# Last expert layer of an eight-block network: the shared expert's up products with the weights stationary over 512 tokens, in high and low parts, and the routing ranks ahead of them

## The chip, the cores and the metric

One core of one Trainium2 chip runs the whole program as a single launch. The metric is device time in microseconds, the median of a few executions; less is better. The engines that matter here are TensorE (PE, with its weight loads shown apart as PEld), VectorE (DVE), ScalarE (ACT), GpSimd (POOL) and SyncE (SP, which only issues DMAs). They run side by side and wait for one another through semaphores.

## The reference, cut to what matters

Four times an attention block and a feed-forward block are added to x, each behind a layer norm and a gate. The change touches the last feed-forward block (B S = 1024 tokens of D = 256 features; E = 8 experts, two per token, hidden width 512, and one shared expert that every token passes), and the third and last attention block only in so far as it prefetches.

```python
x = hidden_states.reshape(-1, 256)                     # 1024 tokens, after the layer norm
shared_out = silu_and_mul(x @ shared_gate_up) @ shared_down      # (256 -> 2*512), (512 -> 256)
probs = softmax(x @ gate_w)                            # 8 experts
topk_w, topk_i = top_k(probs, 2);  topk_w = topk_w / sum(topk_w)
combine = sum(one_hot(topk_i, 8) * topk_w[..., None], axis=1)
for wg, wd, cw in experts:                             # 8 of them
    moe_out += cw[:, None] * (silu_and_mul(x @ wg) @ wd)
return moe_out + shared_out
```

`silu_and_mul` splits its input into a gate and an up half of 512 and gives silu(gate) * up.

## The kernel before, in words

`routed` (from L1742) is the last block. Its order is written out by hand: one program for each engine, and semaphores between them. Tokens come in T = 8 tiles of 128. The work on PE is a list of 31 items: n = 0 to 7 are the 8 token tiles through the shared expert, n = 8 to 30 are NT = 23 tiles of 128 rows, each of one routed expert, gathered by expert.

First DVE writes the normalised tokens XE, PE turns them (L1995) into four PSUM banks, ACT and DVE copy these to XTF (features on partitions; it lives in the tensor XN), and PE computes the router's logits LG (L2003). DVE then runs the routing in small steps: softmax, comparisons of all pairs of experts, and then four functions that are threaded between the shared items by the table `BETWEEN`: `rank` (which experts are chosen), `weigh` (their weights), `place` (the row of a table in DRAM, rows3, for each token and choice), `owners` (which expert owns each of the 23 tiles). `rank` feeds a small count on PE (`count`, L2014 and L2016), which `place` needs. When `place` is done, POOL scatters XE to rows3 with 16 indirect DMAs (L1841), and when all have landed SP loads the first six tiles XB from rows3 (L1821). An expert tile can't start before its rows are back.

One item on PE is: `up` (L2027: 4 products, a 128x128 block of tokens as the stationary side and 512 columns of weights moving, plain fp32, into the two PSUM banks GU), `turn_x` of the next tile where that is a routed one (L2036), `down` of the item before (L2054: 4 products with 256 moving columns into DN), and `turn_h` (L2044: 4 transposes of the hidden tile into HP). ACT makes silu of the gate bank (HG, L1865) and DVE multiplies it by the up bank (HF, L1959). `turn_h` is needed since HF has tokens on partitions and `down` wants the hidden features there; ACT copies its result to HT (L1871). `down` of a shared item is added to X (`finish`, L1971); `down` of a routed item is scaled to YB (L1976), and POOL adds it to the output in DRAM by an indirect DMA (L1848), after X itself has been stored (L1824).

In the trace every plain fp32 product stands as two records with a weight load each. So `x8` at L2027 is one item's four products.

All nine weight blocks (the shared one, index E, first; 1.5 MB each) are loaded by SP at the start of the block (L1814, L1816); PE waits for the eighth expert's before the first routed item.

`mm3` (L95 to L97) is used elsewhere in the program: it makes a product from parts, a high part (the value rounded to fp32r, a reduced fp32 format of the matmul) and a low part (what is left of it), by three fp32r matmuls, high x high, high x low, low x high. Each of these is one record.

`plain_attend` (L1135) is attention 2 and 3; on POOL it spreads keys (L1331, L1332), and after that POOL is idle in attention 3.

## Time and profile before

| what | value |
|---|---|
| median of 3 runs | 1010.23 us (1009.95 to 1011.49) |
| the profiled execution's own time | 1009.22 us |
| its span | 1007.4 us |
| PE busy over the span | 933.2 us, 93% |
| the last block (`routed`) | from 796.7 us to the end |
| its shared items on PE (L2027 from XN, first start) | from 805.3 us |
| its first routed item on PE | at 859.4 us |

The span is what the trace covers; 1.8 us lie around it. A time in a view counts from the start of the span. A view of the chain of waits shows the work that ended last, followed back from the end; a timeline shows single instructions of an engine; a view by windows sums busy time and gives the granted clock of TensorE in each stretch (1.00 is full speed). "issue" and "remote" as a releaser mean that the profile has no event of another engine for the end of that wait.

### The profile page before, as it was taken

What the parts mean: (1) busy time and instruction counts of PE and PEld (TensorE: products, weight loads), DVE (VectorE), ACT (ScalarE), POOL (GpSimd) and SP (SyncE); (2) the same over time, 40 slices, a digit from 0 to 9 for tenths busy, and PEclk for the clock granted to TensorE, in tenths of its full rate; (3) what the DMA queues carried; (4) which work ended last, traced back from release to release, by engine and by line L of the source; (5) the groups of instructions that cost most, each with busy time, mean ns of one, the idle gap of its engine ahead of it and who ended that gap; (6) DMA issues with size and microseconds to landing.
All of it is one profiled execution on the core that took longest, in us unless ns stands there. A gap on an engine that the chain in (4) does not pass through costs nothing. (4 is left out here: it accounts for less than half of the span.)

```text
span 1007.4 us, 15178 instructions
## 1 busy us (share of the span) xinstructions
PE 933.2 (93%) x5006; PEld 696.5 (69%) x5022; DVE 571.2 (57%) x1069; ACT 345.4 (34%) x612; POOL 424.3 (42%) x341
## 2 busy tenths in 40 slices
PE   7999998988899999999979988898799898999996
PEld 4899996966566666667758966786378654666554
DVE  6788886668343443443579887677777451222221
ACT  3454543410033333343424435344154231212111
POOL 5787883030378888674402230530350014122222
PEclk9999999987899999999989999999999899999999
DMA  8321110049345445656520010100000294222210
GB/s 306 129 83 52 44 44 1 2 162 409 96 78 86 77 74 84 148 76 169 170 84 1 2 37 0 38 1 1 11 1 1 95 428 162 57 43 43 36 30 10
DMA packets 38595, 84.84 MB, mean 84 GB/s; under 512 B 9741, under 2 KB 27533, under 8 KB 36014
## 3 DMA queue, kind: packets, MB, share of 16 engines
q1 hardware_dynamic: 22062, 64.56, 18.3%
q0 software_dynamic: 16176, 19.31, 11.6%
q8 instruction: 41, 0.67, 0.3%
q14 instruction: 28, 0.23, 0.1%
q10 hardware_dynamic: 288, 0.07, 0.0%
HBM read 71.23 MB, written 20.68 MB: 91 GB/s over the span
## 5 line engine op out<-in xcount | busy, mean ns | idle before, releaser
L2546 PE MATMUL ffn_GU<-ffn_W,ffn_XTB 128*128 x252 | 90.0, 479 | 3.0 <-DVE ffn_XTB L2451 1.9
L1848 POOL DMA_INDIRECT out_x<-ffn_YB,ffn_XB x23 | 35.8, 1557 | 119.2 <-DVE ffn_YB L1976 117.2
L2027 PE MATMUL ffn_GU<-ffn_W,ffn_XTB 128*128 x184 | 85.0, 605 | 0.0
L2253 POOL DMA_INDIRECT kept_MARKED<-scratch_rows,kept_IDX x63 | 62.4, 991 | 52.3 <-DMA scratch_rows<-ffn_WEIGHT 33.4
L2435 DVE TENSOR_TENSOR ffn_GB<-ffn_GU,ffn_BIAS 128x352 f32<-128x352 f32 x63 | 33.1, 525 | 86.6 <-PE ffn_GU L2546 72.5
L2546 PEld LDWEIGHTS ffn_GU<-ffn_W,ffn_XTB 128*128 128x128 f32 x252 | 43.2, 189 | 35.5 <-issue 21.2
L2054 PE MATMUL ffn_DN<-ffn_W,ffn_HT 128*128 (+1 forms) x248 | 60.3, 387 | 5.6 <-issue 4.9
L2577 PE MATMUL ffn_DN<-ffn_W,ffn_HT 96*128 x252 | 64.8, 379 | 0.0
L2291 ACT ACTIVATE ffn_HG<-ffn_GB 128x176 f32<-128x176 f32 x63 | 22.0, 350 | 115.9 <-DVE ffn_GB L2435 70.0
L1965 DVE COPY ffn_XTB<-ffn_XP 128x256 f32<-128x256 f32 x23 | 9.8, 425 | 86.6 <-PE ffn_XP L2036 86.6
L2027 PEld LDWEIGHTS ffn_GU<-ffn_W,ffn_XTB 128*128 128x128 f32 x184 | 33.1, 189 | 36.0 <-issue 33.6
L2054 PEld LDWEIGHTS ffn_DN<-ffn_W,ffn_HT 128*128 128x128 f32 x248 | 46.0, 193 | 14.7 <-issue 9.6
L356 POOL TENSOR_TENSOR attn_RP<-attn_RP,attn_RS 128x512 f32<-128x512 f32 x32 | 40.6, 1290 | 33.8 <-DVE attn_RS L523 33.8
L1865 ACT ACTIVATE ffn_HG<-ffn_GU 128x512 f32<-128x512 f32 x31 | 18.5, 597 | 88.2 <-PE ffn_GU L2027 84.5
L2577 PEld LDWEIGHTS ffn_DN<-ffn_W,ffn_HT 96*128 96x128 f32 x252 | 43.0, 190 | 3.5
L351 POOL TENSOR_TENSOR attn_WS_lo<-attn_W,attn_WS_hi 128x896 fp32r<-128x896 f32 (+2 forms) x24 | 41.6, 1746 | 5.2 <-ACT attn_WS_hi L427 5.2
L1084 POOL TENSOR_TENSOR attn_PROB<-XN,attn_SM 128x1024 f32<-128x1024 f32 x8 | 15.2, 1904 | 61.3 <-DVE attn_SM L1107 61.3
L95 PE MATMUL attn_QB<-attn_XT_hi,attn_C_hi 128*128 128x512 f32 x96 | 38.5, 401 | 2.3 <-DVE attn_XT_lo L565 2.3
L1871 ACT ACTIVATE ffn_HT<-ffn_HP 128x512 f32<-128x512 f32 x31 | 18.5, 597 | 62.7 <-PE ffn_HP L2044 51.9
L97 PE MATMUL attn_QB<-attn_XT_hi,attn_C_lo 128*128 128x512 f32 x96 | 37.5, 391 | 0.0
L96 PE MATMUL attn_QB<-attn_XT_lo,attn_C_hi 128*128 128x512 f32 x96 | 37.5, 391 | 0.0
L1959 DVE TENSOR_TENSOR ffn_HF<-ffn_GU,ffn_HG 128x512 f32<-128x512 f32 x31 | 21.4, 692 | 26.2 <-ACT ffn_HG L1865 23.2
(529 smaller groups left out, 2520.1 us busy)
## 6 DMA issues: line engine op xcount, KB each, us to landing
ffn_W<-in_f_w SPq DMA_DIRECT2D x9, 1536.0 KB, 6.2
ffn_W<-in_f_w SPq DMA_DIRECT2D x16, 608.0 KB, 18.3
attn_W<-in_L_pairs SPq DMA_DIRECT2D x7, 1088.0 KB, 4.9
scratch_rows<-in_rows_empty SPq DMA_DIRECT2D x1, 2967.0 KB, 13.2
ffn_XB<-scratch_rows SPq DMA_DIRECT2D x23, 129.0 KB, 2.1
ffn_BIAS<-in_f_bias SPq DMA_DIRECT2D x1, 2816.0 KB, 15.3
kept_STAGE<-in_f_w SPq DMA_DIRECT2D x1, 2048.0 KB, 9.6
kept_STAGE<-in_L_pairs SPq DMA_DIRECT2D x2, 768.0 KB, 9.5
```

The source lines that it names most:

```text
L95: pe.matmul(out, a[0], b[0], start=first, stop=False)
L96: pe.matmul(out, a[0], b[1], start=False, stop=False)
L97: return pe.matmul(out, a[1], b[0], start=False, stop=last)
L351: pool.tensor_tensor(WS[1][:, SECTIONS[c]], W[:, SECTIONS[c]], WS[0][:, SECTIONS[c]].bitcast(F32), ALU.subtract).then_inc(w_lo[c], 1)
L356: pool.tensor_tensor(RP[:, q, g, :], RP[:, q, g, :], RS[:, g, 1 - q, :], ALU.add).then_inc(rope_add, 1)
L1848: pool.indirect_dma_start(out[:, :], bass.IndirectOffsetOnAxis(ap=XB[:, i % NB, D:D + 1].bitcast(I32), axis=0), YB[:, i % 3, :], None, bou ...
L2027: last = pe.matmul(GU[:, m, :], x, weights(e, k * 2 * HID3 + m * HID3, HID3), start=k == 0, stop=k == KD - 1)
L2054: last = pe.matmul(DN[:, n % 2, 0:D], HT[:, n % 2, c * P:(c + 1) * P], weights(e, UPW + c * D, D), start=c == 0, stop=c == HID3 // P - 1)
L2253: pool.indirect_dma_start(XB[:, i % NB, :], None, DR["rows0"][:, :], bass.IndirectOffsetOnAxis(ap=IDX[:, i:i + 1], axis=0)).then_inc(rows_ ...
L2435: dve.tensor_tensor(GB[:, n % 2, :], GU[:, n % 2, 0:2 * HID], BIAS[:, bass.ds(e * (2 * HID), 2 * HID)], ALU.add).then_inc(biased, 1)
L2546: last = pe.matmul(GU[:, n % 2, 0:2 * HID], XTB[:, i % 2, k * P:(k + 1) * P], flat[:, bass.ds(e * WIDTH0 + k * 2 * HID, 2 * HID)], start=k ...
L2577: last = pe.matmul(DN[:, n % 2, 0:D], HT[0:rows, n % 2, j * P:(j + 1) * P], w, start=j == 0, stop=j == len(parts) - 1)
```

## The change

1. The shared expert's up weights (128x2048 fp32) are no longer part of W. They are loaded (RAW) at the start of attention 3's block by SP, and split into a high and a low part by two POOL instructions after POOL's last key work there. The parts lie in the space of a tensor, STAGE, that is free by then. W keeps the 8 experts; the shared down weights (128x1024) are a tile of their own, WD.
2. XT, high and low parts of the turned tokens: ACT writes four high parts from the PSUM banks (128x512 each), POOL the four low parts.
3. A shared step is no longer a token tile. There are 8 steps s = 4 h + c: half h of the tokens (512) and chunk c (128) of the hidden features. The weights' 128x128 blocks are stationary, 512 tokens move, in `mm3` form: 2 banks x 2 feature chunks x 3 = 12 matmuls. The result has hidden features on partitions, so `turn_h` and the copy to HT go for the shared part. Two pairs of banks alternate, GU and HP with XP. The hidden tiles are kept in eight places that are free at that time (XB, HF, CMP, HT).
4. `shared_down(t)` is as `down` was: 4 fp32 products with 256 columns per token tile.
5. Order on PE: steps 0, 1, the count, steps 2, 3; then four times a step and one `shared_down`; then four `shared_down`; then `turn_x(8)` and the routed items. On DVE `rank` comes ahead of the first product with silu, and `place` ahead of the third. SP loads XB only after four `shared_down` too.
6. The first routed item has no `down` of an item before it, and `turn_x(8)` has no `up` beside it.

The diff, without the parts that only rename or redirect (waits counted from T, sizes of tiles):

```diff
-        def plain_attend(... normalised=0):
+        def plain_attend(... normalised=0, next_shared=None):
...
+                    else:
+                        @block.sync
+                        def _(sp):
+                            next_shared["load"](sp)
...
+                        if next_shared:
+                            next_shared["halve"](pool)
...
+        def shared_weights(ctx, PARTS):
+            RAW = sbuf(ctx, "RAW", [P, KD * 2 * HID3])
+            loaded, halves = sem(ctx, "shared_loaded"), sem(ctx, "shared_halves")
+            def load(sp):
+                sp.dma_start(RAW[:, :], A["f3_w"][E3][:, 0:KD * 2 * HID3]).then_inc(loaded, 16)
+                sp.wait_ge(loaded, 16)
+            def halve(pool):
+                pool.wait_ge(loaded, 16)
+                pool.tensor_copy(PARTS[0], RAW[:, :]).then_inc(halves, 1)
+                pool.wait_ge(halves, 1)
+                pool.tensor_tensor(PARTS[1], RAW[:, :], PARTS[0].bitcast(F32), ALU.subtract).then_inc(halves, 1)
...
+                HIDDEN = [LATER[:, c * HALF:(c + 1) * HALF] for c in range(3)] + [HF[:, :], CMP[:, 0, :], CMP[:, 1, :], HT[:, 0, :], HT[:, 1, :]]
+                PAIRS = ((GU[:, 0, :], GU[:, 1, :]), (HP[:, :], XP[:, :]))
...
-                        sp.dma_start(W[:, E, :], A["f3_w"][E]).then_inc(shared_in, 16)
+                        sp.dma_start(WD[:, :], A["f3_w"][E][:, UPW:WIDTH]).then_inc(shared_in, 16)
...
                         sp.wait_ge(scattered, 16 * 2 * T)
+                        sp.wait_ge(down_done, T // 2)
...
+                        for j in range(4):
+                            pool.wait_ge(xt_b if j % 2 else xt_a, j // 2 + 1)
+                            pool.wait_ge(xt_hi, j + 1)
+                            pool.tensor_tensor(XT[1][:, j % 2, half(j)], XTF[:, j % 2, half(j)], XT[0][:, j % 2, half(j)].bitcast(F32), ALU.subtract).then_inc(xt_lo, 1)
...
-                        for j in (0, 2):
+                        for j in range(4):
                             act.wait_ge(xt_turned, j + 1)
-                            act.activation(XTF[:, 0, half(j)], NBANK[j], ACT.Copy).then_inc(xt_a, 1)
+                            if j % 2 == 0:
+                                act.activation(XTF[:, 0, half(j)], NBANK[j], ACT.Copy).then_inc(xt_a, 1)
+                            else:
+                                act.wait_ge(xt_b, j // 2 + 1)
+                            act.activation(XT[0][:, j % 2, half(j)], NBANK[j], ACT.Copy).then_inc(xt_hi, 1)
...
-                        BETWEEN = {0: rank, 1: weigh, 2: place, 3: owners}
+                        rank()
+                        shared_full(0)
+                        weigh()
+                        shared_full(1)
+                        place()
+                        shared_full(2)
+                        shared_full(3)
+                        owners()
...
+                        def shared_up(s):
+                            h, c = divmod(s, 4)
+                            pe.wait_ge(xt_hi, 2 * h + 2)
+                            pe.wait_ge(xt_lo, 2 * h + 2)
+                            if s >= 2:
+                                pe.wait_ge(h_full, s - 1)
                             for m in range(2):
                                 for k in range(KD):
+                                    at = slice(k * 2 * HID3 + m * HID3 + c * P, k * 2 * HID3 + m * HID3 + (c + 1) * P)
+                                    last = mm3(pe, PAIRS[s % 2][m], (WS[0][:, at], WS[1][:, at]),
+                                               [x[:, k, h * HALF:(h + 1) * HALF] for x in XT], first=k == 0, last=k == KD - 1)
+                            last.then_inc(up_done, 1)
+                        def shared_down(t):
+                            h, q = divmod(t, T // 2)
+                            pe.wait_ge(h_full, 4 * h + 4)
+                            if t >= 2:
+                                pe.wait_ge(shared_added, t - 1)
+                            for c in range(HID3 // P):
+                                last = pe.matmul(DN[:, t % 2, 0:D], HIDDEN[4 * h + c][:, q * P:(q + 1) * P], WD[:, c * D:(c + 1) * D], start=c == 0, stop=c == HID3 // P - 1)
+                            last.then_inc(down_done, 1)
...
+                        shared_up(0)
+                        shared_up(1)
+                        count()
+                        shared_up(2)
+                        shared_up(3)
                         pe.wait_ge(shared_in, 16)
+                        for s in range(4, T):
+                            shared_up(s)
+                            shared_down(s - 4)
+                        for t in range(4, T):
+                            shared_down(t)
+                        pe.wait_ge(experts_ready, 1)
+                        turn_x(T)
+                        pe.wait_ge(w_in, 16 * E)
```

How instructions stand on PE at the start of the shared part, before the change (LG are the logits, GU the bank pair of `up`, HP the turned hidden tile, PF the count):

```order
L2003 MATMUL ffn_LG<-ffn_RW,XN 128x8 x16
L2027 MATMUL ffn_GU<-ffn_W,XN 128x512 x4
L2044 MATMUL ffn_HP<-IDENT,ffn_HF 128x128 x4
L2027 MATMUL ffn_GU<-ffn_W,XN 128x512 x4
L2054 MATMUL ffn_DN<-ffn_W,ffn_HT 128x256 x4
L2014 MATMUL ffn_PF<-ffn_CHOSEN,ffn_TRI 128x72
```

And there after the change (shared_up_11063 and shared_up_11064 are the high and the low part of the weights; the three rows L95 to L97 stand four times for one step, twice on each bank of its pair):

```order
L2060 MATMUL ffn_LG<-ffn_RW,XN 128x8 x16
L95 MATMUL ffn_GU<-ffn_XT_hi,shared_up_11063 128x512
L96 MATMUL ffn_GU<-ffn_XT_lo,shared_up_11063 128x512
L97 MATMUL ffn_GU<-ffn_XT_hi,shared_up_11064 128x512
...
L95 MATMUL ffn_HP<-ffn_XT_hi,shared_up_11063 128x512
...
L97 MATMUL ffn_XP<-ffn_XT_hi,shared_up_11064 128x512
L2069 MATMUL ffn_PF<-ffn_CHOSEN,ffn_TRI 128x72
```

The transposes HP and the `down` between the first two items are gone, and the second step, on HP and XP, stands right behind the first one.

On DVE, from the last comparison (CMP) to the slots, before the change (HF is the product with silu, PR and XE the ranks and weights, TE and SLOT the placing):

```order
L1914 TENSOR_TENSOR ffn_CMP<-ffn_PR 128x512
L1959 TENSOR_TENSOR ffn_HF<-ffn_GU,ffn_HG 128x512
L1918 TENSOR_TENSOR ffn_CMP<-ffn_CMP,ffn_BEFORE 128x512
L1919 TENSOR_TENSOR ffn_CMP<-ffn_CMP 128x512
L1920 TENSOR_REDUCE ffn_PR<-ffn_CMP 128x64
L1922 TENSOR_SCALAR ffn_CHOSEN<-ffn_PR 128x64
L1959 TENSOR_TENSOR ffn_HF<-ffn_GU,ffn_HG 128x512
L1971 SCALAR_TENSOR_TENSOR X<-ffn_DN,GATE,X 128x256
L1925 SCALAR_TENSOR_TENSOR ffn_PR<-ffn_PR 128x64
```

And after the change (the first product with silu now goes to space of XB):

```order
L1956 TENSOR_TENSOR ffn_CMP<-ffn_PR 128x512
L1960 TENSOR_TENSOR ffn_CMP<-ffn_CMP,ffn_BEFORE 128x512
L1961 TENSOR_TENSOR ffn_CMP<-ffn_CMP 128x512
L1962 TENSOR_REDUCE ffn_PR<-ffn_CMP 128x64
L1964 TENSOR_SCALAR ffn_CHOSEN<-ffn_PR 128x64
L1999 TENSOR_TENSOR ffn_XB<-ffn_GU,ffn_HG 128x512
L1967 SCALAR_TENSOR_TENSOR ffn_PR<-ffn_PR 128x64
```

`rank` has moved ahead of the first product, and between `rank` and `weigh` one product stands where there were a product and a sum into X.

On PE where the routed items begin, before the change:

```order
L2027 MATMUL ffn_GU<-ffn_W,XN 128x512 x4
L2036 MATMUL ffn_XP<-IDENT,ffn_XB 128x128 x2
L2054 MATMUL ffn_DN<-ffn_W,ffn_HT 128x256 x4
L2044 MATMUL ffn_HP<-IDENT,ffn_HF 128x128 x4
L2063 TENSOR_LOAD ffn_EI
L2063 ISA x2
L2027 ISA
L2027 MATMUL ffn_GU<-ffn_W,ffn_XTB 128x512
```

And after it:

```order
L97 MATMUL ffn_XP<-ffn_XT_hi,shared_up_11064 128x512
L2093 MATMUL ffn_DN<-ffn_WD,ffn_XB 128x256 x3
L2093 MATMUL ffn_DN<-ffn_WD,ffn_HF 128x256
L2093 MATMUL ffn_DN<-ffn_WD,ffn_CMP 128x256 x2
L2093 MATMUL ffn_DN<-ffn_WD,ffn_HT 128x256 x2
...
L2112 MATMUL ffn_XP<-IDENT,ffn_XB 128x128 x2
L2149 TENSOR_LOAD ffn_EI
L2149 ISA x2
L2101 ISA
L2101 MATMUL ffn_GU<-ffn_W,ffn_XTB 128x512
```

The transposes XP of the first routed tile now stand behind all shared work, right before the product that needs them; before, they stood ahead of a `down` and a `turn_h`.

## Rows read from the trace of the kernel before

**Rows 1.** Chain that ended last, last block: start us, us, what.

```profile
805.48 5.25 PE ffn_GU L2027 x8
...
812.86 3.44 PE ffn_GU L2027 x8
816.29 1.73 PE ffn_DN L2054 x8
...
844.56 4.87 issue
849.44 3.48 PE ffn_DN L2054 x8
...
859.38 3.70 PE ffn_GU L2027 x8
863.08 0.22 PE ffn_XP L2036 x2
...
865.02 0.44 PE ffn_HP L2044 x4
865.46 3.58 PE ffn_GU L2027 x8
```

**Rows 2.** Timeline of ACT and DVE: start us, us, instruction [idle before <-releaser].

```profile
811.45 0.69 DVE L1959 TENSOR_TENSOR ffn_HF<-ffn_GU,ffn_HG 128x512 f32<-128x512 f32 x1 [3.08 <-ACT ffn_HG L1865]
...
845.24 0.48 DVE L1971 SCALAR_TENSOR_TENSOR X<-ffn_DN,GATE,X 128x256 f32<-128x256 f32 x1 [4.92 <-issue]
848.79 0.60 ACT L1871 ACTIVATE ffn_HT<-ffn_HP 128x512 f32<-128x512 f32 x1 [9.19 <-remote]
```

**Rows 3.** Windows: us, busy us (instructions) PE, PEld, DVE, ACT, POOL, PEclk, DMA, GB/s.

```profile
805.30:810.70 5.40, 5.40 (x10) 2.05 (x9) 2.52 (x8) 1.54 (x2) 0.00 (x0) 0.68 1.00 422
812.80:844.60 31.80, 31.76 (x118) 18.60 (x116) 11.48 (x34) 7.77 (x11) 13.20 (x14) 1.00 0.82 336
849.40:853.60 4.20, 4.16 (x13) 3.36 (x14) 1.18 (x2) 0.61 (x2) 0.00 (x0) 0.59 0.57 150
```

**Rows 4.** Timeline of PE in attention 3, second and last of 24 fp32r products.

```profile
735.43 0.40 PE L96 MATMUL attn_TR<-layer_XT_lo,kept_WQ_hi 128*128 128x512 f32 x1
...
740.57 0.40 PE L97 MATMUL attn_OP<-layer_XT_hi,kept_WQ_lo 128*128 128x512 f32 x1
```

**Rows 5.** Timeline of DVE: first and last instruction of rank, weigh and place.

```profile
812.06 0.68 DVE L1918 TENSOR_TENSOR ffn_CMP<-ffn_CMP,ffn_BEFORE 128x512 f32<-128x512 f32 x1
814.22 0.20 DVE L1922 TENSOR_SCALAR ffn_CHOSEN<-ffn_PR 128x64 bf16<-128x64 f32 x1
818.46 0.22 DVE L1925 SCALAR_TENSOR_TENSOR ffn_PR<-ffn_PR 128x64 f32<-128x64 f32 x1
820.15 0.29 DVE L1933 TENSOR_REDUCE ffn_XE<-ffn_WEIGHTS 128x16 f32<-128x128 f32 x1
824.33 0.16 DVE L1937 TENSOR_SCALAR ffn_TE<-ffn_PF 128x8 f32<-128x8 f32 x1
826.42 0.17 DVE L1947 CAST ffn_SLOT<-ffn_SLOTF 128x16 int32<-128x16 f32 x1
```

**Rows 6.** Timeline of POOL and SP: first and last of 16 scatters, loads of XB.

```profile
827.44 1.03 POOL L1841 DMA_INDIRECT scratch_rows<-ffn_XE,ffn_SLOT  x1 [26.97 <-DVE ffn_SLOT L1947]
...
846.62 0.97 POOL L1841 DMA_INDIRECT scratch_rows<-ffn_XE,ffn_SLOT  x1 [0.30 <-issue]
849.09 3.89 SPq L1821 DMA_DIRECT2D ffn_XB<-scratch_rows  x6
```

**Rows 7.** The tile XB, the load that was issued at 849.09 us.

```profile
DMA to landing us min/median/max: 2.2/2.2/2.2
```

**Rows 8.** POOL's own DMA queue, 831 to 832 us: packets, MB, share.

```profile
q0 software_dynamic: 11, 0.05, 11.3%
```

**Rows 9.** Waits of POOL: instruction <- what it waited for: us, times, longest.

```profile
POOL ffn_ONEB L1829 <- POOLq L1184: 47.9, 1, 47.9
```

**Rows 10.** The page, costliest groups: xcount | busy us, mean ns | idle before.

```profile
L356 POOL TENSOR_TENSOR attn_RP<-attn_RP,attn_RS 128x512 f32<-128x512 f32 x32 | 40.6, 1290 | 33.8 <-DVE attn_RS L523 33.8
```

More of the change, by code:

```diff
@@ L1132, in _, with plain_attend @@
                         add(T - 1)
-        def plain_attend(tag, gate, CW, QO, MASKH, CWS, WQ, VB, following=None, next_weights=None, normalised=0):
+        def plain_attend(tag, gate, CW, QO, MASKH, CWS, WQ, VB, following=None, next_weights=None, normalised=0, next_shared=None):
             with ExitStack() as ctx:
@@ L1739, in _, with routed @@
                         keep_busy(pe, SP[:, :], 20)
-        def routed(gate):
+        def routed(gate, WS):
             E, NT, NB, ROW = E3, TILES3, 6, ROW3
@@ L1746, in routed @@
             with ExitStack() as ctx:
-                W = sbuf(ctx, "W", [P, E + 1, WIDTH])
+                W = sbuf(ctx, "W", [P, E, WIDTH])
+                WD = sbuf(ctx, "WD", [P, WIDTH - UPW])
+                XT = split(ctx, "XT", [P, KD, B * S])
                 XE = sbuf(ctx, "XE", [P, 2, T, ROW])
@@ L2017, in count, with up @@
                             last.then_inc(counted, 1)
-                        def up(n, e):
-                            if n > 0:
-                                pe.wait_ge(h_full, n)
-                            if n >= T:
-                                pe.wait_ge(x_out, n - T + 1)
+                        def shared_up(s):
[4 more added lines that the diff above has]
+                                pe.wait_ge(h_full, s - 1)
                             for m in range(2):
                                 for k in range(KD):
-                                    x = XTF[:, k, n * P:(n + 1) * P] if n < T else XTB[:, n % 2, k * P:(k + 1) * P]
-                                    last = pe.matmul(GU[:, m, :], x, weights(e, k * 2 * HID3 + m * HID3, HID3), start=k == 0, stop=k == KD - 1)
+                                    at = slice(k * 2 * HID3 + m * HID3 + c * P, k * 2 * HID3 + m * HID3 + (c + 1) * P)
[10 more added lines that the diff above has]
+                            last.then_inc(down_done, 1)
+                        def up(n, e):
+                            pe.wait_ge(h_full, n)
+                            pe.wait_ge(x_out, n - T + 1)
+                            for m in range(2):
+                                for k in range(KD):
+                                    last = pe.matmul(GU[:, m, :], XTB[:, n % 2, k * P:(k + 1) * P], weights(e, k * 2 * HID3 + m * HID3, HID3), start=k == 0, stop=k == KD - 1)
                             last.then_inc(up_done, 1)
@@ L2683, in program @@
         phase[0] = "ffn3_"
-        routed(7)
+        routed(7, SHARED)
 def rope_table(length, dim):
```

72 lines of the change are left out of this document (42 added, 30 removed).

## The prediction

> **What bounds the kernel now.** I read the chain of waits first. In the last block it is PE nearly all the way: an item's `up` takes 3.44 us, its `down` 1.73, its transposes 0.44 [rows 1], and PE was busy 31.76 of 31.80 us from 812.80 to 844.60 at full clock [rows 3]. So every matmul that goes from the shared part shortens the path. Two pieces of the chain are not of that kind. The first item took 5.25 us, at a mean granted clock of 0.68 [rows 1, 3]: part of it ran at 1.2 GHz. And at 844.56 PE stood still for 4.87 us, with "issue" as the reason, after which one `down` took 3.48 instead of 1.73 us, at a mean clock of 0.59 [rows 1, 3].
>
> Then I read the timeline of ACT and DVE beside that gap. The waiting `down` needed HT, which ACT wrote at 848.79 after an idle time of 9.19 us put down to "remote"; DVE's sum into X came at 845.24 after 4.92 us, put down to "issue" [rows 2]. PE's matmuls that both wait for stood in the chain ahead of 844.56 [rows 1]. So two engines got on late by several microseconds for a reason that the trace doesn't name. It falls into the time of the scatters, 827.44 to 847.59 [rows 6]. I call it the hiccup; with its slow clock it costs 4.87 + (3.48 - 1.73) + about 0.2 for the transposes behind it = 6.8 us.
>
> Last, the routing, which isn't on the path but must be ready for the first routed item: the slots were ready at 826.59 [rows 5], the scatters ran from 827.44, SP issued the XB loads at 849.09 [rows 6], and the first landed 2.2 us later [rows 7], at 851.3. PE came to that item at 859.38 [rows 1]: 8 us of slack.
>
> **The change part by part.** I compare the stretch of PE from 805.48 to 865.46, the start of the second routed `up` [rows 1]: 59.98 us. Behind it nothing is changed.
>
> Before, in that stretch: `up` 5.25 + 7 x 3.44 = 29.33; `up` of the first routed item 3.70; `down` 8 x 1.73 = 13.84; transposes of hidden tiles 9 times, 8 x 0.44 and 0.9 more for the slower ones, 4.4; `turn_x` 2 x 0.22; count 0.2; the wait of the first item for silu and product, 810.73 to 812.20, 1.4; the hiccup's 4.87 + 1.75. Sum 59.9.
>
> Step (a), the products. An fp32r product of 128x512 starts every (740.57 - 735.43) / 22 = 0.234 us [rows 4]. A step has 12, so 2.80 us; eight would take 22.4. A token tile's `up` had 8 records of 0.43. That is three passes in place of four, less the pitch's 0.02 each. The first step begins slow, as the first item did: that was 5.25 - 3.44 = 1.81 us late, so some 3.6 us ran at the lower level. In 3.6 us go 8 products of 0.43 (half rate), then 4 of 0.234: 4.5 us. All: 4.5 + 7 x 2.80 = 24.1, against 29.3. Gain 5.2.
>
> Step (b), what goes with the turned layout: eight groups of transposes (3.8 us) and the wait of 1.4 us, which the second pair of banks fills with step 1. Gain 5.3.
>
> Step (c), the downs: 8 x 1.73, the stationary side and the 256 columns are as before. `shared_down(3)` (1.73 us) covers silu (0.60) and product (0.69) of the last step [rows 2], which `shared_down(4)` needs: with two hand-overs of 0.06 that is 1.4 us, so nothing waits. Each `shared_down` waits for the sum into X two before it, 0.48 us of DVE [rows 2] in 1.73. Nought.
>
> Step (d), what is added at the border. `turn_x(8)` has no `up` beside it: the transposes (0.22 [rows 1]), the copy XTB (as long as DVE's other 128x256 pass, 0.48 [rows 2]) and two or three hand-overs of 0.06 make 0.85 us, 0.65 more than 0.22. The first routed item has no `down` behind it to cover silu and product: 1.4 us. Its `up` is 3.65, 0.05 less than before. Loss 2.0.
>
> Step (e), the hiccup. If it is gone, 6.8 us more.
>
> New stretch: 24.1 + 13.84 + 0.2 + 0.85 + 3.65 + 0.22 + 1.4 + 0.44 = 44.7. The gain is 59.98 - 44.7 = 15.3 us, of which 8.5 are work and bubbles and 6.8 the hiccup.
>
> Step (f), are the rows back? DVE is idle for 3.08 us before 811.45 [rows 2], so `rank` can start at 808.4. It takes 2.36 us (812.06 to 814.42), `weigh` 1.98 (818.46 to 820.44), `place` 2.26 (824.33 to 826.59) [rows 5]. PE ends step 0 at about 810.0, step 1 at 812.8, the count at 813.0. DVE: `rank` to 810.8, product to 811.5, `weigh` to 813.5, product 1 to 814.2, `place` to 816.5. That is 10 us earlier than 826.59. The scatters keep POOL 20.15 us plus 0.85 before, as in rows 6: last issue over at 837.5. SP issued the XB loads 1.5 us after that [rows 6], so 839.0, and the first lands at 841.2. PE is through its shared work at 805.48 + 24.1 + 0.2 + 13.84 = 843.6. So rows are there 2.4 us early: PE still sets the time, though the slack has shrunk from 8 us. SP's added wait, for four `shared_down`, is over at about 836.6, before the scatters are. What is queued behind it on SP are only the XB loads and the store of X.
>
> The scatters now fall into the load of the expert weights. There only 11 packets with 0.05 MB went through POOL's queue in one microsecond [rows 8], while a scatter is 0.13 MB and is issued every 1.28 us. From both sides: with no slowing the loads are issued at 839.0. If no scatter moves until the weights are in, 2.1 MB follow behind them. The weights are about 14 MB, 1 MB less than before, at 422 GB/s and a DMA share of 1.00 [rows 3], so in at about 831; the 2.1 MB take 5 us at that rate and 10 at half of it, and the loads are issued between 839 and 842.5. I take 839.0, since the issue by POOL, one in 1.28 us, was the slower part before. At the upper end the first tile lands at 844.7 and PE waits 1.1 us.
>
> The Trainium skill, DMA: Bandwidth & Descriptors, section Queues, rings and completion order, says that each DMA engine serves its queues in turn, packet by packet. By that rule the scatters are neither shut out nor ahead; the sum would stay at 839. The trace agrees as far as both queues moved packets in the same microsecond [rows 8].
>
> Step (g), edits at nothing. The load of RAW and POOL's two instructions of 128x2048 lie in attention 3, where POOL was idle for 47.9 us before this block [rows 9]; they need about 10 us of it, by elements from POOL's 128x512 pass of 1.29 us [rows 10]. If DVE were slowed by them, as two engines at the same memory can be, it could cost up to their own 10 us; DVE's softmax steps are on that block's path. I take 0. ACT's four and POOL's four new passes before the first step run beside the logits (801.9 to 805.5): ACT, at 0.60 a pass, is done at about 803.5, and the two low parts that step 0 needs, at 1.29 us each [rows 10] from about 801, at 803.6. I take 0; if that cover is gone, 1 us.
>
> **Forecast.** Span 1007.4 - 15.3 = 992.1; with the 1.8 us around it 993.9. The median of the runs shown, 1010.23, is 1.0 above the profiled execution; so 995.
>
> **The rivals.**
> A. The hiccup stays. It came while scatters were under way [rows 2, 6], and these are all still there. For it: two engines were late at once for no reason in the program, so the cause is outside the instructions that moved. Against: it came once in 16 scatters, and the change moves the scatters to a time in which PE does other things. In the new order most PE work of that time doesn't need ACT (four `shared_down` in a row), so it may also be partly hidden. Time: 995 + 6.8 = 1001.8 at most. Chance 0.33.
> B. The rows come late and PE waits at `turn_x(8)`: the scatters are stretched beyond the bound above, or POOL is held up by a full queue. For it: before, 6 scatters had been issued when the weights were in, now 11 or 12 will be. If POOL could issue only one in 2 us until 831, 9 would be left, over at 843, and the rows land at 846.7: 3 us of waiting, and a slow clock behind it as at 849.44 (another 1.9). Against: POOL's gap of 0.30 us stayed the same under the load [rows 6]. Time 995 + 5 = 1000. Chance 0.10.
> C. On the other side: PE's clock. If the new order leaves PE at the lower level, each product takes 0.43 us, 2.36 us more for a step, and each `shared_down` 3.48 instead of 1.73 [rows 1]. Over the whole shared part that is 7 x 2.36 + 8 x 1.75 = 30.5 us, and the time 1025. It decides from half of it on: over 15 us of loss, or some 31 us of the stretch at the lower level, is slower than before. Against: from 812.80 on the clock was 1.00 with PE as dense as it will be [rows 3]. For: the first item's 0.68 shows that the level is low on entry [rows 3]. Chance 0.04. The Trainium skill, TensorE: Matmul & The Clock Gate, section Part 1: The HAM clock gate, calls the throttled state the default that activity releases; by it the sum stays, since activity doesn't fall.
> D. The products don't run at the pitch of rows 4, or the split costs attention 3 up to its 10 us: 995 + 4 to 10, up to 1005. Chance 0.06.
> The forecast itself, hiccup gone or hidden: 0.47, with its own range 992.5 to 997.5.
>
> **How the numbers follow.** A, B and D lie between 999 and 1003, the forecast between 992.5 and 997.5. From 992 to 1002.5 I leave out C, the worst of D, and some below. Faster by over 0.2% (about 2 us, what can be told from no change here) is all but C and mishaps: 0.95; no change 0.01; slower 0.04.
>
> **What would show it.** In the changed profile: L95 to L97 on GU, HP and XP at a start-to-start of 0.23 us, 96 in all; the first scatter at 817 to 818 and the XB loads at 839; the first routed `up` at about 844.5 and the second near 850; the slots at about 816.5; clock 1.00 from 810 on; no idle PE over 1.5 us after that. Any gap of PE over 3 us with "issue" or "remote" on ACT or DVE is rival A; a wait of `turn_x(8)` for XB is B; L95 to L97 at 0.4 us beyond the first step is C; longer DVE steps in attention 3 are D. If the stretch to the second routed `up` is over 48 us without such a gap, my sum is wrong.

## The result, and the profile after

| what | value |
|---|---|
| median of 13 runs | 1002.68 us (1000.30 to 1008.75) |
| the kernel before, 13 runs | 1011.33 us (1008.94 to 1018.39) |
| ratio | 0.9922, 95% interval 0.9903 to 0.9941 |
| the profiled execution's own time, its span | 1000.98 us, 999.2 us |

Faster by 8.7 us, not by the 15.3 that were forecast; 1002.68 lies just above the range's end of 1002.5, and 0.9 above rival A's 1001.8. (The 13 runs of before have a median 1.1 us above that of the three runs that the forecast started from.) I call *the stretch* what the prediction compared: PE from the first shared product to the start of the second routed `up`. Before it took 59.98 us [rows 1]. After the change it is 55.3 us, where 44.7 were forecast.

The chain of waits of the changed kernel (start us, us, what) answers to rows 1:

```profile
802.14 0.63 PE ffn_GU L95
802.76 0.43 PE ffn_GU L96
...
807.03 0.43 PE ffn_GU L97
...
824.56 0.70 DVE ffn_CMP L1999
825.30 12.50 another core or an unknown queue
837.83 0.61 ACT ffn_HG L1903
...
839.87 0.70 DVE ffn_HT L1999
840.62 9.65 PE ffn_DN L2093 x32
...
851.35 3.69 PE ffn_GU L2101 x8
...
857.31 3.70 PE ffn_GU L2101 x8
```

Two things are to be seen. The first step's products start 0.43 us apart, where those of rows 4 are 0.234 us apart: half the rate. And the chain leaves PE for 12.5 us, for something that the profile has no name for. The timeline of PE, ACT and DVE of the same time shows what it was (start us, us, instruction [idle before <-releaser]):

```profile
828.26 1.46 PE L2093 MATMUL ffn_DN<-ffn_WD,ffn_XB 128*128 128x256 f32 x6
834.97 0.38 PE L2093 MATMUL ffn_DN<-ffn_WD,ffn_HF 128*128 128x256 f32 x1 [0.53 <-issue]
840.62 2.08 PE L2093 MATMUL ffn_DN<-ffn_WD,ffn_CMP 128*128 128x256 f32 x4 [5.27 <-DVE ffn_HT L1999]
842.48 1.91 PE L2093 MATMUL ffn_DN<-ffn_WD,ffn_HT 128*128 128x256 f32 x4
851.35 3.69 PE L2101 MATMUL ffn_GU<-ffn_W,ffn_XTB 128*128 x8 [0.88 <-DVE ffn_XTB L2011]
```

```profile
837.83 0.60 ACT L1903 ACTIVATE ffn_HG<-ffn_GU 128x512 f32<-128x512 f32 x1 [13.30 <-remote]
```

```profile
827.17 0.48 DVE L2017 SCALAR_TENSOR_TENSOR X<-ffn_DN,GATE,X 128x256 f32<-128x256 f32 x1 [1.92 <-remote]
838.46 0.69 DVE L1999 TENSOR_TENSOR ffn_HT<-ffn_GU,ffn_HG 128x512 f32<-128x512 f32 x1 [10.80 <-ACT ffn_HG L1903]
```

PE had finished the products of step 6 at 828.26, where its `shared_down` begins. ACT made their silu only at 837.83, 9.6 us later, as "remote". PE went on with step 7 and `shared_down(3)`, and then stood still for 5.27 us. That is rival A: the hiccup came back, at another instruction. It again lies in the time of the scatters; POOL was through with issuing them at 835.14, 2.7 us ahead of the late silu:

```profile
814.97 1.03 POOL L1875 DMA_INDIRECT scratch_rows<-ffn_XE,ffn_SLOT  x1 [12.11 <-DVE ffn_SLOT L1989]
...
834.17 0.97 POOL L1875 DMA_INDIRECT scratch_rows<-ffn_XE,ffn_SLOT  x1 [0.30 <-issue]
```

```profile
838.18 2.70 SPq L1851 DMA_DIRECT2D ffn_XB<-scratch_rows  x6
```

These two answer to rows 6: scatters and loads of XB 12.5 and 10.9 us earlier than before. The windows answer to rows 3 (us, busy us of PE, PEld, DVE, ACT, POOL, then PEclk, DMA share, GB/s):

```profile
802.00:807.30 5.30, 5.30 (x14) 4.14 (x15) 4.82 (x12) 1.54 (x2) 0.87 (x1) 0.50 1.00 420
808.00:830.00 22.00, 22.00 (x105) 17.91 (x105) 9.64 (x30) 4.90 (x7) 11.68 (x12) 1.00 1.01 423
840.50:845.80 5.30, 5.18 (x13) 4.17 (x14) 0.93 (x3) 0.00 (x0) 0.00 (x0) 0.52 0.31 95
```

PE is full and at full clock from 808, and at the 1.2 GHz level in the first step and again behind the gap.

### The profile page after: what moved, and what is told of

The parts are those of the page before. It is cut to its first block and busy times, and to the rows that moved or that the text cites. A ratio compares the mean times of both kernels' runs of the same rounds, so it can differ in the third digit from the quotient of the medians.

```text
span 999.2 us, 15175 instructions
## 1 busy us (share of the span) xinstructions
PE 923.0 (92%) x5006; PEld 698.2 (70%) x5022; DVE 570.5 (57%) x1069; ACT 342.5 (34%) x608; POOL 435.2 (44%) x347
## 5 line engine op out<-in xcount | busy, mean ns | idle before, releaser
L1903 ACT ACTIVATE ffn_HG<-ffn_GU 128x512 f32<-128x512 f32 x27 | 16.1, 597 | 102.5 <-PE ffn_GU L2101 81.2
L2130 PE MATMUL ffn_DN<-ffn_W,ffn_HT 128*128 x184 | 43.6, 380 | 0.8 <-ACT ffn_HT L1911 0.8
L95 PE MATMUL attn_QB<-attn_XT_hi,attn_C_hi 128*128 128x512 f32 x96 | 38.5, 401 | 2.3 <-DVE attn_XT_lo L565 2.3
L97 PE MATMUL attn_QB<-attn_XT_hi,attn_C_lo 128*128 128x512 f32 x96 | 37.5, 391 | 0.0
L2130 PEld LDWEIGHTS ffn_DN<-ffn_W,ffn_HT 128*128 128x128 f32 x184 | 33.2, 190 | 5.0 <-issue 1.5
L444 ACT ACTIVATE attn_U<-attn_TR 32x768 f32<-32x768 f32 x32 | 25.7, 804 | 20.8 <-PE attn_TR L657 20.2
L2623 PE MATMUL ffn_GU<-kept_STAGE 128*128 128x352 f32 x64 | 27.2, 557 | 5.2 <-DVE ffn_HFS L2529 3.1
```

Of the source, the lines that this page charges most:

```text
L95: pe.matmul(out, a[0], b[0], start=first, stop=False)
L97: return pe.matmul(out, a[1], b[0], start=False, stop=last)
L2130: last = pe.matmul(DN[:, n % 2, 0:D], HT[:, n % 2, c * P:(c + 1) * P], weights(e, UPW + c * D, D), start=c == 0, stop=c == HID3 // P - 1)
```

## The experiments

Each study of up to four kernels had its own runs of the kernel before beside them. The kernels f5 and f6 ran in the study of g1 and g2. In four studies (the result, and the kernels e, g and i) these runs had medians of 1009.3 to 1011.3 us, in two (f1 to f4, and h) 1002.5 and 1001.8. That matters below. For each trace I give the stretch too, since it leaves out what varies ahead of it.

### Do the scatters make the signals late? (e1 to e4)

```diff
                         for k in range(2):          # e1, e2: range(0); e3: range(1)
+                        pool.wait_ge(up_done, 6)    # e4 alone, ahead of the loop
```

e1 and e2 leave all 16 scatters out of the changed kernel and of the kernel before, e3 the second eight; SP then waits for the experts or for eight scatters. The rows that are not scattered are missing from the output.

> The changed kernel without its 16 scatters to rows3 (the routed tiles are then loaded from rows that hold no token, so the routed part of the output is left out; SP loads XB once the tiles' owners are known). Theory S (while scatters are under way, what PE signals to ACT and DVE reaches them late, and that is the gap): ACT's silu of step 6 follows the end of its products by under 0.1 us, PE has no gap over 1.5 us before the second routed up, which starts some 47 us after the first step; total 6 to 8 us below the changed kernel, about 993 to 995. Theory T (the gap comes from the weight load or from something at that place of the program): gap and total unchanged, about 1001 to 1003.

> The kernel before without its 16 scatters (the same part left out). S: the 4.87 us gap and the 3.48 us down behind it are gone, 6 to 7 us below the kernel before. T: unchanged.

> The changed kernel with the 8 scatters of the first choice only (half of the routed rows left out). S, if the delay needs many scatters or a long series: in the full kernel the first late signal came 10 us after the first scatter, when 9 had been issued, so with 8 there is none or one of a few us, and the total is 5 to 8 us below the changed kernel. S, if any scatter delays: part of the gap, 2 to 4 us less than in full. T: unchanged.

> The changed kernel with POOL's first scatter held until step 5 is done, about 824 instead of 815 us. S: the late signals move with the scatters: silu of step 6 at about 828.5 is on time, late ones begin after 834 and end with the last landing near 846; rows land near 849. T: silu of step 6 is still about 9 us late.

| kernel | median us | ratio to before | stretch us |
|---|---|---|---|
| before | 1011.15 | 1 | 60.0 (first trace) |
| e2, before without scatters | 1000.36 | 0.9884 (0.9839 to 0.9928) | 53.9 |
| e1, after without scatters | 993.49 | 0.982 (0.9777 to 0.9864) | 46.0 |
| e3, after with eight | 994.98 | 0.9837 (0.9799 to 0.9876) | 45.4 |
| e4, after, scatters 9.6 us later | 1002.38 (one run) | none | 56.3 |

Without scatters the hiccup is gone from both kernels. The chain of e1, where the one above left PE:

```profile
831.25 1.73 PE ffn_DN L2093 x8
...
835.77 8.65 PE ffn_DN L2093 x40
...
845.50 3.69 PE ffn_GU L2101 x8
...
851.47 3.69 PE ffn_GU L2101 x8
```

In e4 the scatters run from 824.58 to 844.73. Steps 6 and 7 now get their silu in time, and three sums into X are late instead, behind two waits; its timeline of DVE:

```profile
834.54 0.48 DVE L2018 SCALAR_TENSOR_TENSOR X<-ffn_DN,GATE,X 128x256 f32<-128x256 f32 x1 [0.41 <-PE ffn_DN L2094]
840.15 0.48 DVE L2018 SCALAR_TENSOR_TENSOR X<-ffn_DN,GATE,X 128x256 f32<-128x256 f32 x1 [5.12 <-remote]
847.18 0.88 DVE L2018 SCALAR_TENSOR_TENSOR X<-ffn_DN,GATE,X 128x256 f32<-128x256 f32 x2 [6.55 <-remote]
```

So the hiccup belongs to the scatters, moves with them, and takes whichever signal of PE falls into it. With eight of them one sum into X was 0.7 us late and nothing else. It isn't the weights' load: in e4 no packet of that queue is left after 828, and the late signals came from 835 on.

### Pauses, short rows, plain products (f1 to f4, h1 to h3)

```diff
+                            if k == 1:                                        # f1, h1
+                                pool.wait_ge(scattered, 16 * T)
+                                if t % 4 == 0 and k * T + t > 0:              # f2
+                                    pool.wait_ge(scattered, 16 * (k * T + t))
-                                pool.indirect_dma_start(DR["rows3"][:, :], ... XE[:, k, t, :], None)
+                                pool.indirect_dma_start(DR["short"][:, :], ... XE[:, k, t, 0:32], None)   # f3, h2
-                                    last = mm3(pe, PAIRS[s % 2][m], (WS[0][:, at], WS[1][:, at]), ...)
+                                    last = pe.matmul(PAIRS[s % 2][m], WS[0][:, at].bitcast(F32), XTF[...], ...)   # f4, h3
```

> The changed kernel with a pause: POOL issues 8 scatters, waits until all 8 have landed, then issues the other 8. With 8 alone the signals were hardly late (0.7 us), with 16 in a row by 9.6. Theory P (the delay builds up with the scatters in a row that have not been worked off, and a pause lets it go): silu of step 6 at about 828.3 and no gap of PE over 1.5 us in the second half either; the pause costs POOL some 2 to 5 us, so the rows come at 843 to 846 and PE waits 0 to 3 us for them: 994 to 998. Theory N (from the ninth scatter on signals are late whatever the spacing, a matter of their number in the queue): a late silu or sum of 5 to 10 us again, 1001 to 1005.

> The changed kernel with three pauses: POOL issues scatters in groups of 4 and waits each time until all issued so far have landed. Theory P: no late signal at all; three waits of 2 to 5 us each put the last scatter at 843 to 850 and the first routed up at 848 to 855, so PE waits 4 to 10 us for rows: 998 to 1004. Theory N: late signals of 5 to 10 us from the ninth scatter on, in part under PE's wait for rows: 1002 to 1010.

> The changed kernel with 16 scatters of the same 128 rows each, but of 32 elements instead of 258, to a table of their own; the routed rows stay empty, so the sums by indirect DMA at the end find no token, as in the run without scatters. Theory B (the bytes on their way delay the signals): an eighth of the bytes, no late signal, 993 to 995. Theory D (the descriptors, 128 a scatter, or POOL's making of them): the same late silu and sum of 8 to 10 us, 1001 to 1003.

> The changed kernel with step (a) undone: a shared step is 4 plain fp32 products (8 records) of the high part of the weights with XTF instead of 12 fp32r products. The low part of the weights is left out of the computation. By step (a) of the prediction each of 8 steps is 3.44 instead of 2.80 to 2.82 us: the stretch 5.0 us longer less what the late signals hide of it. If the sum is right and the hiccup stays: 1005 to 1008. Rival: PE waits so long on the late signals that part of the longer products is covered, 1003 to 1005.

In f3 and h2 the routed rows stay empty, so the routed part is missing from the output; f4 and h3 leave out the low part of the weights.

| kernel | median us | ratio to before (1002.48) | stretch us |
|---|---|---|---|
| f1, one pause | 999.12 | 0.9967 (0.9953 to 0.9981) | 52.7 |
| f2, three pauses | 1002.80 | 1.0012 (0.9994 to 1.0029) | 58.4 |
| f3, short rows | 990.04 | 0.9876 (0.9853 to 0.9898) | 45.4 |
| f4, plain products | 997.14 | 0.995 (0.9928 to 0.9971) | 51.5 |

f2 shows rows later still, a wait of 9.7 us. None of the four traces has a late signal, not even f4's, with 16 full scatters in a row. And before ran 1002.48 here. So in this study f1 to f3 can't say what removes the hiccup. What they do show is the price of waiting for rows. In f1 the eighth scatter was issued at 823.73 and POOL waited 8.43 us for it to land, with the weights still coming; the rows were then late. The chain of f1:

```profile
837.87 3.45 PE ffn_DN L2095 x16
841.32 5.39 issue
846.71 0.67 PE ffn_XP L2114 x2
...
848.08 5.23 PE ffn_GU L2103 x8
```

5.39 us of waiting, and 5.23 instead of 3.69 for the next `up`, whose products begin at the slow pitch. This is rival B's mechanism, brought about by hand.

I ran three of them again, hoping for a study like the first.

> The kernel of f1 once more, for a chip on which before runs near 1010 us. Theory P (the delay builds up with the scatters in a row): no wait of ACT or DVE on remote or issue over 1.5 us, rows back 3 to 5 us late as in f1, 996 to 1000, ratio 0.987 to 0.990. Theory N (from the ninth on, whatever the spacing): late signals again in the second eight, in the time after 840, under PE's wait for rows or on top of it, 1000 to 1006, ratio 0.991 to 0.996.

> The kernel of f3 once more (16 scatters of 32 elements a row; the routed rows stay empty). On a chip where before runs near 1010 us. Theory B (bytes): no late signal, 991 to 995, ratio 0.981 to 0.985. Theory D (number of scatters and descriptors): late silu and sum by 8 to 10 us as in the changed kernel, 999 to 1003, ratio 0.989 to 0.993.

> The kernel of f4 once more (plain fp32 products of the high part of the weights, low part left out). If f4 was free of late signals because of its chip: on a chip where before runs near 1010 they are here, and the time is 1004 to 1008, up to 5.0 above the changed kernel (0.64 us for each of 8 steps). If it was free because of its products: none here either, 997 to 1000.

Measured: 997.77 (ratio 0.9964, 0.995 to 0.9978), 990.95 (0.9876, 0.9839 to 0.9913), 998.32 (0.9957, 0.9936 to 0.9978), with before at 1001.81; stretches 52.7, 45.4, 50.7. The same picture a second time, again without late signals. Bytes against number of scatters thus stays open.

f4 and h3 do settle step (a). Their chains have a step of 3.43 us (8 records) where the changed kernel has 2.81; the line of f4 and one of h3:

```profile
830.01 3.43 PE ffn_GU L2083 x8
```

```profile
832.01 3.43 PE ffn_GU L2083 x8
```

Eight steps make 5.0 us. The stretches are longer by 6.1 and 5.3 (51.5 and 50.7 against 45.4 twice). The first step, which begins slowly and took 6.0 and 5.2 us against 4.4, adds 1.0 and 0.2 to the 5.0, which is most of the rest.

### Before and after again, the ranks alone, idle matmuls (g1, g2, f5, f6)

```diff
+                        rank()                                  # f5, in the kernel before
-                        BETWEEN = {0: rank, 1: weigh, 2: place, 3: owners}
+                        BETWEEN = {0: weigh, 1: place, 2: owners}
+                        keep_busy(pe, XP[:, :], 10)             # f6, ahead of the transposes
```

In f5 the count on PE is one item earlier too.

> The kernel before, unchanged, for a second trace. In the study of f1 to f4 it ran 1002.5 us, on another chip than in the first study (1011.2), and the changed kernel with plain products (f4), with all its 16 scatters in a row, showed no late signal. Theory C (the hiccup belongs to the chip as well as to the scatters): on a chip where before runs near 1002 its trace has no idle PE of 4 to 5 us near the fifth shared item and no remote wait of ACT over 3 us; on one where it runs near 1010 both are there. Theory R (it comes by run, and the clocks make the 9 us): the hiccup in some executions, and no tie to the time.

> The changed kernel, unchanged. Theory C: without the hiccup (before near 1002) it gains what the work gives, 8.5 us by the prediction and 6.9 by the first study's runs without scatters: 993 to 996, with the first shared up to the second routed up in 45 to 46 us. With the hiccup (before near 1010) 1002 to 1003 and 55 us as in the first trace. Theory R: somewhere between, the stretch 45 or 55 us by chance.

> The kernel before with the ranks ahead and nothing else: rank comes ahead of the first product with silu, the count on PE one item earlier, weigh and place one item earlier each. The scatters begin some 4 us sooner. By the prediction the rows had 8 us of slack, so the ranks alone are worth nothing: same as before, ratio 0.998 to 1.002. The first product with silu waits 2.4 us for rank, which delays the second up: rival, slower by 1 to 2.4 us, ratio 1.001 to 1.003. Where the hiccup is on this chip, it moves 4 us ahead and costs the same.

> The changed kernel with 10 idle matmuls on PE while it waits for the normalised tokens, ahead of the transposes. In the trace of the changed kernel the first 12 products ran at half clock, 5.3 us instead of 2.8. Theory W (the level of the clock at the first step is set by how little PE did in the wait): full clock in step 0, 2.0 to 2.5 us faster than the changed kernel. Rival: the clock falls anyway, since the transposes and logits are small, 0 to 0.5 us slower.

| kernel | median us | ratio to before (1009.33) | stretch us |
|---|---|---|---|
| g1, before | 1008.78 | 0.9994 (0.9977 to 1.0011) | 59.5 |
| g2, after | 1002.96 | 0.9939 (0.992 to 0.9958) | 52.9 |
| f5, before with ranks ahead | 1010.48 | 1.0011 (0.9992 to 1.0029) | 59.9 |
| f6, after with idle matmuls | 998.98 | 0.9897 (0.9873 to 0.9921) | 52.0 |

All four traces have the hiccup. In g1 PE stood still for 2.8 us and, a `down` later, for 0.8; the chain of g1, before:

```profile
838.12 0.45 PE ffn_HP L2044 x4
838.62 3.41 issue
842.06 4.80 another core or an unknown queue
846.86 2.85 issue
849.74 3.53 another core or an unknown queue
```

The timeline of ACT of g2, after:

```profile
835.58 0.60 ACT L1903 ACTIVATE ffn_HG<-ffn_GU 128x512 f32<-128x512 f32 x1 [11.08 <-remote]
837.88 0.60 ACT L1903 ACTIVATE ffn_HG<-ffn_HP 128x512 f32<-128x512 f32 x1 [1.71 <-remote]
```

The ranks alone are worth nothing, as step (f) had it: the rows weren't what PE waited for. In f5 the first scatter was issued at 823.46, 4.0 us sooner than in the first trace of before [rows 6], and PE's gap, of 4.2 us, began at 840.59, 4.0 us sooner as well [rows 1]: once more the hiccup moved with the scatters.

f6 also shows which signals are late. DVE took up ACT's silu of 831.38 at 832.01, 0.03 us after its end, while DVE's next sum, which waits for PE, came only at 837.76. So between ACT and DVE signals were in time. Whether PE sent its own late or the others received them late isn't shown.

f6 is 4 us below the changed kernel in the medians, and the two intervals just meet. Its windows from the transposes to the end of the first step:

```profile
797.40:803.00 5.60, 5.60 (x50) 5.29 (x48) 2.49 (x6) 4.43 (x7) 3.88 (x5) 1.00 0.87 289
803.00:808.50 5.50, 5.50 (x26) 4.45 (x25) 5.05 (x11) 3.92 (x4) 1.42 (x2) 1.00 1.01 425
```

And the same of g2:

```profile
795.60:802.00 6.40, 5.90 (x48) 5.67 (x49) 2.79 (x8) 4.43 (x7) 4.35 (x6) 0.94 0.83 277
802.00:807.50 5.50, 5.50 (x14) 4.34 (x15) 4.96 (x12) 1.54 (x2) 0.92 (x1) 0.50 1.02 430
```

26 matmuls in 5.5 us instead of 14. In the two runs of h4 and i2 below, with the same idle matmuls, transposes and logits were at full clock too, but the clock of the 5 us behind them was 0.67: the first step is not always saved. What the idle matmuls had in common is the piece ahead of it: from the transposes to the first product it was 5.5 us in all three traces with them (f6, h4, i2). In the 17 without it was 5.9 (e3, f1 to f3, h1 to h3), 6.3 to 7.0 (before, after, g2, i1) or 10.0 us (e1, e2, e4, f4, f5, g1), 7.5 on average. By these figures I estimate the worth of the idle matmuls at 2.0 us there, and 2.5 more where the first step was at full clock.

### A version that avoids the hiccup (h4, i1, i2)

```diff
                         for e in range(E):
+                            if e == E - 2:
+                                sp.wait_ge(scattered, 16 * T)
                             sp.dma_start(W[:, e, :], A["f3_w"][e]).then_inc(w_in, 16)
```

with the pause of f1 and the idle matmuls of f6.

> The changed kernel with three things: the pause of f1; SP holds back the last two experts' weights (3 MB) until the first 8 scatters have landed; 10 idle matmuls ahead of the transposes as in f6. In f1 the first 8 landed only 9.4 us after the eighth was issued, since the weights were still coming; here they should land 2 to 4 us after it, the second 8 are out by 837 to 839, and rows and weights are in before PE needs them at 843. Theory P: no late signal, no wait for rows, 991 to 994. Theory N: 999 to 1003. Rival: the weights come late, and PE waits for them at the first routed product, 995 to 999.

> The changed kernel, unchanged. Where before runs near 1002: the hiccup is absent from both kernels if it is what separates the studies, then only the work gain of 8.5 us is left (6.9 in the runs without scatters): 993 to 996, ratio 0.991 to 0.994, and the stretch from the first shared up to the second routed up is 45 to 47 us with no late signal. Where before runs near 1010: 1002 to 1003, ratio 0.992 to 0.994, late silu of 9 to 11 us and a stretch of 53 to 56 us, as twice already. Rival: near 1002 the changed kernel has late signals all the same and gains nothing, ratio 0.998 to 1.002.

> The kernel of h4 once more (pause, last two experts' weights held back until 8 scatters have landed, 10 idle matmuls). Where before runs near 1010: theory P (a pause lets the delay go) no late signal over 1.5 us, 994 to 997, 6 to 8 us below the changed kernel; theory N, late signals in the second eight, 999 to 1003. Where before runs near 1002: no late signals in either, so what is left is the clock of the first step (2.5 us gained) against the wait for rows and the slow first routed up (2.8 and 1.5 us lost in h4): within 2 us of the changed kernel.

| kernel | median us | ratio to before | stretch us |
|---|---|---|---|
| h4 | 994.88 | 0.9929 (0.9907 to 0.9951) of 1001.81 | 49.7 |
| i1, the changed kernel | 1001.70 | 0.9931 (0.991 to 0.9953) of 1009.85 | 53.4 |
| i2, the kernel of h4 | 999.51 | 0.989 (0.9857 to 0.9924) of 1009.85 | 51.9 |

For h4, 991 to 994 were expected without a wait for rows; PE waited 2.8 us for them, and the next `up` took 5.20 us, so it missed by 0.9. The last study was one with the hiccup: i1's silu of step 6 is late as in the first trace.

```profile
836.25 0.60 ACT L1903 ACTIVATE ffn_HG<-ffn_GU 128x512 f32<-128x512 f32 x1 [13.20 <-remote]
```

i2, in the same study, has no late signal over 1.0 us (one sum into X). Its chain:

```profile
829.06 1.73 PE ffn_DN L2098 x8
833.58 8.76 PE ffn_DN L2098 x40
842.34 3.53 issue
845.87 0.67 PE ffn_XP L2117 x2
...
847.24 6.26 PE ffn_GU L2106 x8
```

All eight `shared_down` and silus pass without a gap, with 16 scatters. What it wins there it mostly gives back: the pause still takes POOL 4.02 us, the loads of XB are issued at 843.63, PE waits 3.53 us for them and makes the next `up` in 6.26 instead of 3.69. That is 6.1 us, against 8.7 of the hiccup. The forecast of 994 to 997 missed for that reason. i2 is 2.2 us below i1 in the medians, and their intervals overlap, so it isn't shown to be faster than the changed kernel; nor is it faster than f6. It differs from the changed kernel in three things; the idle matmuls don't remove the hiccup (f6), but the pause and the held-back weights aren't told apart. In the other kind of study, h4 is the lowest of the kernels that compute everything (994.88; h1 997.77), by 2.9 us.

## Why the prediction was wrong

By the profiled executions the span was forecast at 992.1 and was 999.2: 7.1 more. Where they lie, from the rows above and the PE timeline between them:

| piece | forecast us | measured us | off by |
|---|---|---|---|
| ahead of the stretch (start of the first product) | 805.3 | 802.0 | -3.3 |
| steps 0 and 1, count | 7.5 | 8.7 | +1.2 |
| steps 2 to 7 and downs 0 to 2 | 22.0 | 22.1 | +0.1 |
| down 3, the gap, downs 4 to 7 | 8.65 | 2.57 + 5.27 + 9.47 = 17.3 | +8.7 |
| `turn_x`, XTB | 0.85 | 1.26 | +0.4 |
| first routed item | 5.7 | 5.96 | +0.25 |
| behind the stretch | 142.05 | 141.9 | -0.15 |

**Step (e) failed.** I took the hiccup's 6.8 us as gone, with a chance of 0.47 for that against 0.33 for rival A. The runs show why this was the wrong way round: the cause is the scatters (e1 to e4), and all 16 were still there. "It came once in 16 scatters" was no evidence against it: in all eight traces of those four studies with 16 scatters in a row it is there, some 10 to 13 us after the first one. Its size was off as well: 8.7 us in the first trace (0.84 + 5.27 + 2.55: down 3 stretched, the gap, downs 4 to 7 slow), and about 7 in g2 and i1 by their stretches against e1's 46.0. "At most" 6.8 was therefore no bound. That "most PE work of that time doesn't need ACT" held for step 7 and down 3 alone; downs 4 to 7 need the silus of 6 and 7.

**The work gain was right.** I forecast 8.5 us without the hiccup. Without scatters the stretch is 53.9 before and 46.0 after: 7.9, and the medians, of four runs each, differ by 6.9. The pitch (0.233 to 0.234 us, a step 2.81), the downs at 1.73, the added 2 us at the border (2.6 measured) and the second pair of banks all came as written. The stretch of 46.0 against my 44.7 is the next two points.

**Step (a), the first step.** I let the 1.2 GHz level last 3.6 us, from the first item of before. It lasted from 802.0 to about 808.1 here, through the whole first step and two products of the second. Cost 1.2 us with the count.

**Step (d), the border.** XTB's copy waited for the last sum into X on DVE, which stands ahead of it; I had forgotten that instruction. 0.4 us.

**Step (f), the rows.** The slots were ready at 814.1 (forecast 816.5), the scatters began at 814.97 and XB was issued at 838.18 (839.0): POOL's issue pitch of 1.27 us held under the load. That 838.18 lies so near 839.0 is luck, since everything began 3.3 us early. Counted from the first product, XB was issued after 36.2 us, where 33.7 were forecast. The slots account for 0.9 of that. The other 1.5 are SP's: it waits for the scatters and for PE's fourth `shared_down`, and went on 3.0 us after the last scatter's issue instead of 1.5, by a wait that is put down to "remote". POOL's queue moved its last packets between 836 and 837, and `shared_down(3)` was over at 835.35, so SP's signal from PE was most likely late too. By the time that the weights were in, near 832, 14 scatters had been issued, not 11 or 12, and POOL had not been held up once; rival B's condition wasn't met, and f1 shows what it would have cost. In f1 eight scatters issued by 824.7 had landed by 833.1, beside the weights: from 824 to 830, at a DMA share of 1.01, POOL's queue moved 182 packets with 0.52 MB and SP's 181 with 2.00 MB. The Trainium skill (DMA: Bandwidth & Descriptors, Queues, rings and completion order) says that an engine goes round its queues packet by packet; the equal numbers of packets agree with that.

**Step (g).** Attention 3 didn't grow, 66.7 us from its start to the first transposes against 68.4 before; and DVE's steps kept their length: the softmax pass of 128x1024 took 1224 ns, 1225 before. C didn't come true: the clock was full from 808.1 until the gap. Nor did D: the products ran at the pitch of rows 4.

**Ahead of the stretch** 3.3 us were gained that no step of mine claimed: 1.0 up to attention 3, 1.7 in it, 0.7 in transposes and logits. In attention 3 it is seven idle matmuls that took 3.05 us before and 1.67 after. I can't put this down to the change: from the transposes to the first product the traces need 5.9 to 10.0 us, as listed at f6, with or without the change. It is luck, and it hid part of the miss: without these 3.3 us the 1002.68 would have been near 1006, by my estimate. In e1's slow one the mean granted clock was 0.54:

```profile
795.70:805.40 9.70, 9.29 (x48) 9.05 (x48) 2.54 (x6) 4.57 (x7) 5.27 (x6) 0.54 0.90 341
```

What stays open. First, why signals of PE are late in a series of scatters: bytes, descriptors or their number in flight. Second, why two studies show none. The kernels e, which had it, and h, which had none, both ran on a chip with the number 1, so that number doesn't settle it. The kernel before was as fast there (1002.5, 1001.8) as it is without scatters (1000.4), so its hiccup was most likely absent too, but no trace of before or of the changed kernel was taken in such a study. f4 and h3, the only ones there with 16 full scatters in a row, differ from the changed kernel in their products. Third, that a pause removes the hiccup rests on one trace in a study that had it (i2), which also held weights back, beside e3 with eight scatters.

## What to carry to other kernels

A stall that the profile can't name, but that coincides with a transfer, stays as long as the transfer stays: forecast it as moved, not as gone, and price what it can hit in the new order. Leave the instructions out that coincide with it in one run before counting on it either way. And when a stretch is compared, look at the clock level at its entry: a product took 0.43 us at the lower level and 0.23 at the full one. A few idle matmuls ahead of it went with 4 us less in the medians of f6, with intervals that just meet, and didn't keep the first step at full clock in h4 and i2. Last, take a trace of the unchanged kernel in each study: here a stall of 7 to 9 us was there in four studies and most likely absent in two.

## What the hardware showed that was not expected

- Work of ACT and DVE that waited for PE started up to 9.6 us late during a series of 16 indirect scatters of 132 KB each (128 rows of 258 fp32), from 10 to 13 us after the first scatter until shortly after the last packet (packets to between 836 and 837, the late silu at 837.83). DVE's wait for ACT in the same time was not late (0.03 us in f6). Single instructions went through in that time, as DVE's sum at 840.15 between two waits of 5.12 and 6.55 us in e4.
- The same kernel before had medians of 1009.3 to 1011.3 us in four studies and 1001.8 to 1002.5 in two, with 19 or more runs in each of the two, ranges of 999 to 1005 and 998 to 1007.
- A stop of PE costs twice: after 2.8 to 5.4 us of idleness (h4, i2, f1) the next `up` took 5.2 to 6.3 us instead of 3.7, and after 5.27 us the next four `shared_down` 9.5 instead of 6.9.
- Eight scatters issued in 10.0 us had landed 8.4 us after the eighth while weights were loading (f1), and after 4.0 with the last two experts' weights held back (i2). Beside the weights, POOL's and SP's queues moved equal numbers of packets (182 and 181 in 6 us, f1), and so POOL's the fewer bytes (0.52 against 2.00 MB).
